# Perceiver attention: score, mask and exponentiate by pairs of batches, with half slots interleaved

## The chip, the cores and the metric

One core of one Trainium2 chip runs the whole kernel in one launch. The metric is device time in microseconds (us), as the median of several runs. Engines: TensorE (PE; PEld is its weight load), VectorE (DVE), ScalarE (ACT), GpSimd (POOL), and SyncE (SP), which issues the transfers. They run beside each other and meet only at semaphores.

## The reference

Eight layers update x, 32 batches of 128 rows of 128 values, with a context of 32 x 128 x 96. The change lies in the third attention, a Perceiver:

```python
def _L2_xattn_ref(x, latents, mask, ...):          # x: context, latents: layernorm of the running x
    xn = layernorm(x, ln_x_g, ln_x_b)
    ln = layernorm(latents, ln_l_g, ln_l_b)
    q = ln @ Wq.T
    kv = jnp.concatenate([xn @ Wkv.T, ln @ Wlkv.T], axis=1)
    k, v = (kv[..., :INNER], kv[..., INNER:])      # 2 heads of 64
    qn = rmsnorm(q, qn_g) * SCALE
    kn = rmsnorm(k, kn_g)
    attn = jnp.einsum('bhid,bhjd->bhij', qn, kn)   # 128 x 256 per batch and head
    attn = jnp.where(full_mask, attn, -max)
    attn = jax.nn.softmax(attn, axis=-1)
    out = jnp.einsum('bhij,bhjd->bhid', attn, v)
    return out @ Wo.T + bo
x = x + tanh(g_xattn[2]) * _L2_xattn_ref(ctx, _layernorm(x), mask, ...)
```

The other seven layers are cosine attention, soft mixture of experts, 16-head attention, routed experts, then after the Perceiver eight experts, another attention, and a selected GELU.

## The kernel before

The layers follow each other, with a barrier of all engines after each (`end_layer`, L63 to L67). x stays in on-chip memory (`x_resident`) throughout. The diff touches `layer4_perceiver` (L1662) alone.

There the 32 batches form eight groups of four (G = 4). Each engine has a program of its own, written out by hand as a loop over slots, `SLOTS = range(-4, 9)`. In slot t an engine works on several groups at once: statistics of group t+4, normalising and turning (transposing) of the inputs of t+3, projections of t+2, key scaling and turned q and k of t+1, scores and softmax of t, and output of t-1. `there(j)` leaves out groups that don't exist. An engine works strictly in its own order, and a wait stops all behind it.

What each step is, in the names of the profile:

- ScalarE: `keep` (L1868) copies one batch's q, k and v out of `a_project_bank` (rows a_q L1871 and a_kv L1872). `square` (L1874) squares q and k of a group (a_sq, L1879 and L1881). `empty_work` (L1891) copies a turned tile out of `a_work_bank`. `exponentiate` (L1898) does one exponential for each batch and head, eight for a group, with the row sums. `copy_turned_probs` (L1866) copies one batch's turned probabilities.
- VectorE: `mean_squares` (L1767), `scale_keys` (L1779), `mask_scores` (mask L1791 for two batches at a time, maximum L1797, `shift` L1801), `invert_sums` (L1807), `normalise_outputs` (L1812), `update` of x (L1822), and the layer norms in the helper `Norm` (L127 to L147).
- GpSimd: powers to -1/2: key roots (L1737) and query roots (L1739), `rstd` of the latent (L1744) and of the context norm (L140), and the bias added to x (L188).
- TensorE: `turn` (L1946) for q, context, latent, latent keys and context keys, all through the one bank `a_work_bank`; `turn_probs` (L1953); `project` (L1963, L1964), one batch at a time through `a_project_bank`, which `keep` must have emptied; `scores` (L1977); `weigh` (L1987); turned output (L2020) and output product (L2030) in `a_out_bank`.

`a_score_bank` holds the scores of four batches, and the turned probabilities are written to the same places. So `scores(t)` waits until all four of group t-1 have been copied (`pT_done`). In a slot TensorE turns group t-1's probabilities first, and ScalarE exponentiates group t near the end of its slot, before `square(t + 2)`:

```python
                    if there(t):
                        exponentiate(t)
                    if there(t + 2):
                        square(t + 2)
```

Context blocks are loaded by SyncE into one of two buffers as soon as the context norm has used it (L1725).

## Time and profile before

| | |
|---|---|
| median of 3 runs | 2292.95 us (2291.43 to 2298.33) |
| profiled execution, its own time | 2296.02 us |
| its span | 2294.2 us |
| TensorE / VectorE / ScalarE / GpSimd busy | 2004.6 / 1571.2 / 1250.2 / 796.4 us |
| mean granted clock of TensorE | 0.922 |
| Perceiver stage, first work to last update | 1360.6 to 1577.7 us |
| next layer's first VectorE row | 1578.77 us |

A row of a timeline gives the start in us from the span's start, the duration in us, the engine, the line, the operation, the tile written <- the tiles read, and in brackets how long the engine stood before it and for whom. Rows of one kind in a run are merged (x4). Instructions on one engine are pipelined, so the next starts somewhat before the printed end of the one before; the pitch is from start to start. A row of a stretch gives, for a:b, its length and then the busy us of each engine, and the granted clock (1.00 is 2.4 GHz, 0.50 is 1.2 GHz).

### The profile page before, as it was taken

Reading aid. Unit: us, or ns where it says so; the run is one execution under the profiler, and the core shown is the slowest. Engines: PE = TensorE matmul, PEld = TensorE weight load, DVE = VectorE, ACT = ScalarE, POOL = GpSimd, SP = SyncE. Lnnn points to the kernel's source line nnn. Section 1 sums busy time; section 2 is a strip of 40 time slices with the busy share of each in tenths; the row PEclk is TensorE's granted clock in tenths of the full one; section 3 lists DMA queues with packets and bytes.
Section 4 is the critical chain, followed back from the end, with each engine's and each line's share of the span. In section 5 each row is a group of like instructions: output and inputs, shape, how many; then the busy total and the mean of one; then the engine's idle time right before and its main releaser. Section 6 shows DMA issues by size and latency. Waiting matters only on the chain. (4 is left out here: it accounts for less than half of the span.)

```text
span 2294.2 us, 49158 instructions
## 1 busy us (share of the span) xinstructions
PE 2004.6 (87%) x18068; PEld 1514.7 (66%) x18068; DVE 1571.2 (68%) x3190; ACT 1250.2 (54%) x2832; POOL 796.4 (35%) x698
## 2 busy tenths in 40 slices
PE   6669999999996998969999977777997999999964
PEld 3359999899994666646666644665684666666653
DVE  5789999999997888734544445554575566666644
ACT  3279888888871676723333215754422566666631
POOL 1124445444461333225444444331000333333233
PEclk7589999999997999979999988997998999999975
DMA  2100000000002000044533520001000000000001
GB/s 59 43 1 8 14 9 14 9 14 15 8 8 77 9 9 6 2 92 94 123 81 75 117 42 15 4 1 52 1 1 11 1 4 5 9 4 1 1 2 37
DMA packets 41418, 61.81 MB, mean 27 GB/s; under 512 B 9464, under 2 KB 18208, under 8 KB 40800
## 3 DMA queue, kind: packets, MB, share of 16 engines
q1 hardware_dynamic: 41184, 58.66, 10.6%
q8 instruction: 151, 2.47, 0.5%
q14 instruction: 83, 0.68, 0.1%
HBM read 56.02 MB, written 2.62 MB: 26 GB/s over the span
## 5 line engine op out<-in xcount | busy, mean ns | idle before, releaser
L827 POOL TENSOR_TENSOR a_probs<-a_probs,a_rsums 128x1024 f32<-128x1024 f32 x64 | 121.3, 1896 | 321.3 <-DVE a_rsums L875 321.3
L1510 POOL TENSOR_TENSOR f_h<-f_gated,f_w_spread 128x512 f32<-128x512 f32 x128 | 161.6, 1268 | 196.7 <-DVE f_gated L1564 93.7
L1564 DVE TENSOR_TENSOR f_gated<-f_silu,f_up 128x512 f32<-128x512 f32 x128 | 87.1, 686 | 184.3 <-PE f_up L1641 169.4
L2336 ACT ACTIVATE f_combine<-f_logits,f_neg_row_max 128x128 f32<-128x128 f32 x512 | 198.5, 396 | 0.7 <-DVE f_neg_row_max L2194 0.7
L1604 ACT ACTIVATE f_silu<-f_gate 128x512 f32<-128x512 f32 x128 | 76.2, 597 | 221.2 <-PE f_gate L1641 218.0
L2155 POOL TENSOR_TENSOR f_slot_sum<-f_slot_sum,f_logits 128x512 f32<-128x512 f32 x96 | 122.7, 1278 | 182.2 <-DVE f_slot_max L2273 99.1
L2163 POOL TENSOR_TENSOR f_acc<-f_acc,f_row_factor 128x512 f32<-128x512 f32 x128 | 136.2, 1066 | 60.5 <-DVE f_slot_max L2273 38.4
L1656 PEld LDWEIGHTS f_acc<-f_down,f_h 128*128 128x128 f32 x1024 | 128.9, 192 | 42.6 <-issue 37.8
L2397 PE MATMUL f_give_bank<-f_y,f_combineT 128*128 128x128 f32 x1024 | 140.7, 281 | 12.8 <-DVE f_y L2243 7.4
L863 DVE TENSOR_REDUCE a_negmax<-a_score_bank 128x8 f32<-128x1024 f32 x64 | 78.2, 1222 | 102.9 <-PE a_score_bank L1004 102.9
L2386 PE MATMUL f_slot_bank<-f_logits,f_xn 128*128 128x128 f32 x1024 | 136.5, 276 | 6.0 <-issue 5.1
L2424 PE MATMUL f_logit_bank<-f_phi,f_xT 128*128 (+1 forms) x1024 | 137.1, 280 | 3.0 <-ACT f_logits L2316 3.0
L2397 PEld LDWEIGHTS f_give_bank<-f_y,f_combineT 128*128 128x128 f32 x1024 | 125.6, 193 | 20.2 <-DVE f_y L2243 14.9
L1641 PE MATMUL f_gate<-f_xT,f_gate_up 128*128 128x512 f32 x256 | 133.2, 602 | 2.2 <-DVE f_gated L1564 2.2
L2259 DVE TENSOR_TENSOR f_logits<-f_logits,f_neg_slot_max 128x512 f32<-128x512 f32 x128 | 131.6, 1028 | 4.4 <-ACT f_combine L2336 3.4
L1656 PE MATMUL f_acc<-f_down,f_h 128*128 128x128 f32 x1024 | 131.8, 275 | 2.5 <-POOL f_h L1510 2.5
L1641 PE MATMUL f_up<-f_xT,f_gate_up 128*128 128x512 f32 x256 | 131.6, 596 | 0.0
L2386 PEld LDWEIGHTS f_slot_bank<-f_logits,f_xn 128*128 128x128 f32 x1024 | 124.5, 192 | 7.9 <-issue 6.4
L2424 PEld LDWEIGHTS f_logit_bank<-f_phi,f_xT 128*128 128x128 f32 x1024 | 126.9, 196 | 3.6 <-ACT f_logits L2316 3.6
L2374 PE MATMUL f_expert_bank<-f_w,f_slots 128*32 128x128 f32 x4096 | 127.5, 276 | 1.2 <-issue 1.2
L2374 PEld LDWEIGHTS f_expert_bank<-f_w,f_slots 128*32 128x32 f32 x4096 | 109.5, 111 | 9.8 <-issue 2.2
L931 ACT ACTIVATE a_probs<-a_probs 128x1024 f32<-128x1024 f32 x64 | 67.8, 1060 | 70.9 <-DVE a_probs L866 70.9
(327 smaller groups left out, 4997.3 us busy)
## 6 DMA issues: line engine op xcount, KB each, us to landing
f_w_spread<-f_routing_rows SPq DMA_DIRECT2D x64, 512.0 KB, 9.9
f_w<-in_f_w SPq DMA_DIRECT2D x16, 256.0 KB, 2.5
a_cT<-in_ctxT SPq DMA_DIRECT2D x16, 192.0 KB, 2.5
f_gate_up<-in_f_guT SPq DMA_DIRECT2D x1, 2048.0 KB, 8.1
out<-x_resident SPq DMA_DIRECT2D x8, 256.0 KB, 2.4
c_cT<-in_ctxT SPq DMA_DIRECT2D x8, 192.0 KB, 2.5
a_ctx<-in_ctx SPq DMA_DIRECT2D x8, 192.0 KB, 2.6
f_phi<-in_f_phi SPq DMA_DIRECT2D x1, 1024.0 KB, 5.9
```

What stands on the lines that cost most here:

```text
L827: nc.gpsimd.tensor_tensor(probs[:, u], probs[:, u], rsums[:, u, :].unsqueeze(2).to_broadcast([S, 8, S]), ALU.mult).then_inc(normalised, 1)
L1510: nc.gpsimd.tensor_tensor(h[:, u % KEPT, :], gated[:, u % 2, :], w_spread[:, u // PER, u % PER, :], ALU.mult).then_inc(weighted, 1)
L1641: nc.tensor.matmul(ps[step % 2][:, :], gu_w[:, step, k, :], norm.xT[:, s, :], start=True, stop=True).then_inc(done, 1)
L1656: last = nc.tensor.matmul(acc[s][:, j * D:(j + 1) * D], h[:, u % KEPT, j * S:(j + 1) * S], down_w[:, u, :], start=u == 0 and j == 0, stop= ...
L2155: nc.gpsimd.tensor_tensor(slot_sum[:, :, :], slot_sum[:, :, :] if g > 1 else raw[:, (m - 1) % RING], raw[:, m % RING], ALU.add).then_inc(p ...
L2163: nc.gpsimd.tensor_tensor(acc[:, group(g), :], acc[:, group(g), :], factor[:, m // GROUPS % 3, group(g)].unsqueeze(2).to_broadcast([S, G, D]),
L2259: nc.vector.tensor_tensor(e, e, wide(neg_slot[:, m // GROUPS % 3, :]), ALU.add).then_inc(shifts, 1)
L2336: last = nc.scalar.activation(back[:, m % BACKS, j, :], raw[:, m % RING, j, :], ACT.Exp, bias=neg_row[:, k, b:b + 1], accum_out=row_part[: ...
L2374: last = nc.tensor.matmul(expert_banks[m % 2][rows, j * D:(j + 1) * D], slots[:, m % KEPT, j, rows], w_s[:, k, e, :], start=True, stop=True)
L2386: last = nc.tensor.matmul(slot_bank[:, j * CH:(j + 1) * CH], xn[:, g * G + j, :], raw[:, m % RING, j, :], start=True, stop=True)
L2397: last = nc.tensor.matmul(give_banks[m % 2][:, j * D:(j + 1) * D], backT[:, m % TURNED, j, :], y[:, m % KEPT, j, :], start=True, stop=True)
L2424: last = nc.tensor.matmul(logit_banks[m % 2][:, j * CH:(j + 1) * CH], xT[:, g * G + j, :], phi_c[:, c, :], start=True, stop=True)
```

## The change

A group's scores, masks, maxima, shifts, exponentials, turned probabilities and weighing are done for two batches at a time (p = 0, 1) instead of four, with waits to match, and the two halves stand in different places of a slot:

- TensorE scores the first pair of t at the start of slot t and turns its probabilities near the end of the same slot. The second pair is scored in mid-slot and its probabilities turned in slot t+1, behind the first weighing of t. All four projections move, so that a projection stands between most other steps.
- ScalarE exponentiates the first pair of t in mid-slot t and copies its turned probabilities late in that slot. The second pair's exponentials stand first in slot t+1.
- VectorE does the sum of squares first, then mask, maximum and shift of the first pair, then the norms (context ahead of latent), and the second pair's behind the key scaling. The shift of a pair is now its own small multiply.
- GpSimd's query roots of t+1 wait until the exponentials of t-1, which read the same buffer, are done. Before, the key roots ahead of them waited for the shift of t-1. The context norm's `rstd` stands behind the bias add.
- The conversion of the mask (`neg`) stands at the end of slot -2 instead of at the start of slot -1.

The instructions and their shapes are otherwise the same. Nothing of the diff touches another layer or the barrier ahead of the eight experts.

```diff
@@ -1732,10 +1732,10 @@
                     j = t + 1
                     if there(j):
                         pool.wait_ge(ms_done, j + 1)
-                        if j >= 2:
-                            pool.wait_ge(shift_ready, j - 1)
                         nc.gpsimd.tensor_tensor(rn[:, j % 2, 2 * G:], ms[:, 2 * G:], core.minus_half[:, 0:4 * G],
                                                 ALU.pow).then_inc(k_roots, 1)
+                        if j >= 2:
+                            pool.wait_ge(exps, G * (j - 1))
                         nc.gpsimd.tensor_tensor(rn[:, j % 2, 0:2 * G], ms[:, 0:2 * G], core.minus_half[:, 0:2 * G],
                                                 ALU.pow).then_inc(q_roots, 1)
                     if there(t + 4):
@@ -1743,9 +1743,10 @@
                         pool.wait_ge(n_l.veps_done, j + 1)
                         nc.gpsimd.tensor_tensor(n_l.rstd[:, s, :], n_l.veps[:, s, :], core.minus_half[:, 0:G],
                                                 ALU.pow).then_inc(n_l.rstd_done, 1)
-                        n_c.gpsimd_rstd(pool, i, s, j)
                     if there(t):
                         bias.gpsimd_add(pool, at(t), n_l.xn_done)
+                    if there(t + 4):
+                        n_c.gpsimd_rstd(pool, *at(t + 4))
 
             @block.vector
             def _(dve):
@@ -1782,24 +1783,21 @@
                         rn[:, s, 2 * G:].rearrange("p (n h) -> p n h", h=H).unsqueeze(3).to_broadcast([S, 2 * G, H, DH]),
                         ALU.mult).then_inc(kn_done, 1)
 
-                def mask_scores(j):
...
+                def mask_scores(j, p):
+                    s, bs = j % 2, slice(2 * p, 2 * p + 2)
+                    dve.wait_ge(scored, 2 * j + p + 1)
+                    if j >= 2:
+                        dve.wait_ge(flips, 4 * (j - 2) + 2 * p + 2)
+                    nc.vector.tensor_tensor(
+                        sc[:, s, :, bs, :].rearrange("p h b k -> p h (b k)"), score_half(p),
+                        neg[:, 4 * j + 2 * p:4 * j + 2 * p + 2].rearrange("p b c k -> p (b c k)").unsqueeze(1)
+                        .to_broadcast([S, H, 2 * 2 * S]), ALU.add).then_inc(masked, 1)
+                    dve.wait_ge(masked, 2 * j + p + 1)
+                    nc.vector.tensor_reduce(negmax[:, :, bs], sc[:, s, :, bs, :], AX.X, ALU.max, negate=True).then_inc(maxed, 1)
+                    dve.wait_ge(maxed, 2 * j + p + 1)
                     dve.wait_ge(q_roots, j + 1)
+                    nc.vector.tensor_tensor(shift[:, s, bs], negmax[:, :, bs].rearrange("p h b -> p b h"),
+                                            rn[:, s, 4 * p:4 * p + 4].rearrange("p (b h) -> p b h", h=H),
                                             ALU.mult).then_inc(shift_ready, 1)
 
                 def invert_sums(j):
...
@@ -1829,28 +1827,30 @@
                         dve.wait_ge(weights, LOADED)
                         nc.vector.tensor_scalar(q_gain[:, :], vecs[:, 4:5], DH ** -0.5, None, ALU.mult).then_inc(gain_done, 1)
                         bias.vector_start()
-                    if t == -1:
-                        nc.vector.tensor_scalar(neg[:, :, CTX, :], mask_u8[:, :, :], 1.0, MASKED, ALU.subtract, ALU.mult)\
-                            .then_inc(neg_done, 1)
+                    if there(t + 1):
+                        mean_squares(t + 1)
+                    if there(t):
+                        if t == 0:
+                            dve.wait_ge(neg_done, 2)
+                        mask_scores(t, 0)
+                    if there(t + 3):
+                        n_c.vector_normalise(dve, *at(t + 3))
+                        n_l.vector_normalise(dve, *at(t + 3))
                     if there(t - 1):
                         invert_sums(t - 1)
-                    if there(t + 1):
-                        mean_squares(t + 1)
-                    if there(t + 3):
-                        n_l.vector_normalise(dve, *at(t + 3))
-                        n_c.vector_normalise(dve, *at(t + 3))
                     if there(t + 4):
                         latent_statistics(t + 4)
                     if there(t + 1):
                         scale_keys(t + 1)
                     if there(t):
-                        if t == 0:
-                            dve.wait_ge(neg_done, 2)
-                        mask_scores(t)
+                        mask_scores(t, 1)
                     if there(t - 1):
                         normalise_outputs(t - 1)
                     if there(t + 4):
                         context_statistics(t + 4)
+                    if t == -2:
+                        nc.vector.tensor_scalar(neg[:, :, CTX, :], mask_u8[:, :, :], 1.0, MASKED, ALU.subtract, ALU.mult)\
+                            .then_inc(neg_done, 1)
                     if there(t - 1):
                         update(t - 1)
 
@@ -1861,8 +1861,8 @@
 
                 def copy_turned_probs(j, b):
                     act.wait_ge(flips, G * j + b + 1)
-                    if j and b == 0:
-                        act.wait_ge(weighed, j)
+                    if j and b % 2 == 0:
+                        act.wait_ge(weighed, 2 * (j - 1) + b // 2 + 1)
                     nc.scalar.activation(pT[:, b].rearrange("p a k -> p (a k)"), score_bank[:, 512 * b:512 * b + 512],
                                          ACT.Copy).then_inc(pT_done, 1)
 
@@ -1890,10 +1890,10 @@
                         ps = ps.rearrange("p (b k) -> p b k", b=G)
                     nc.scalar.activation(out, ps, ACT.Identity if "bias" in args else ACT.Copy, **args).then_inc(work_emptied, 1)
 
-                def exponentiate(j):
+                def exponentiate(j, p):
                     s = j % 2
-                    act.wait_ge(shift_ready, j + 1)
-                    for b in range(G):
+                    act.wait_ge(shift_ready, 2 * j + p + 1)
+                    for b in (2 * p, 2 * p + 1):
                         for h in range(H):
                             last = nc.scalar.activation(sc[:, s, h, b, :], sc[:, s, h, b, :], ACT.Exp,
                                                         bias=shift[:, s, b, h:h + 1], scale=rn[:, s, b * H + h:b * H + h + 1],
@@ -1902,34 +1902,36 @@
 
                 for t in SLOTS:
                     if there(t - 1):
-                        copy_turned_probs(t - 1, 0)
-                        copy_turned_probs(t - 1, 1)
+                        exponentiate(t - 1, 1)
                     if there(t + 1):
                         empty_work("q", t + 1, qT[:, (t + 1) % 2], scale=q_gain[:, 0:1])
+                    if there(t + 2):
+                        keep(t + 2, 0)
                     if there(t - 1):
                         copy_turned_probs(t - 1, 2)
                         copy_turned_probs(t - 1, 3)
                     if there(t + 2):
-                        keep(t + 2, 0)
+                        keep(t + 2, 1)
                     if there(t + 3):
                         empty_work("c", t + 3, cT[:, (t + 3) % 2, :], bias=vecs[0:C, 1:2], scale=vecs[0:C, 0:1])
                     if there(t + 2):
-                        keep(t + 2, 1)
+                        keep(t + 2, 2)
+                    if there(t):
+                        exponentiate(t, 0)
                     if there(t + 3):
                         empty_work("l", t + 3, lT[:, (t + 3) % 2, :], bias=vecs[:, 3:4], scale=vecs[:, 2:3])
                     if there(t + 2):
-                        keep(t + 2, 2)
+                        keep(t + 2, 3)
+                    if there(t):
+                        copy_turned_probs(t, 0)
+                        copy_turned_probs(t, 1)
                     if there(t + 1):
                         empty_work("k_lat", t + 1, kT[:, (t + 1) % 2, :, LAT, :], scale=vecs[:, 5:6])
                     if there(t - 1):
                         act.wait_ge(o_turned, t)
                         nc.scalar.activation(oT[:, :], out_bank[:, :], ACT.Copy).then_inc(oT_ready, 1)
-                    if there(t + 2):
-                        keep(t + 2, 3)
                     if there(t + 1):
                         empty_work("k_ctx", t + 1, kT[:, (t + 1) % 2, :, CTX, :], scale=vecs[:, 5:6])
-                    if there(t):
-                        exponentiate(t)
                     if there(t + 2):
                         square(t + 2)
 
...
@@ -1964,54 +1966,58 @@
                     nc.tensor.matmul(both[:, CTX, D:3 * D], cT[:, j % 2, bs], wc[:, :], start=True, stop=True)\
                         .then_inc(projected, 1)
 
-                def scores(j):
+                def scores(j, p):
                     s = j % 2
                     pe.wait_ge(work_emptied, use["k_ctx", j] + 1)
                     if j:
-                        pe.wait_ge(pT_done, G * j)
-                    for p in range(2):
-                        for b in (2 * p, 2 * p + 1):
...
-                def weigh(j, b):
-                    pe.wait_ge(pT_done, G * j + b + 1)
+                        pe.wait_ge(pT_done, G * (j - 1) + 2 * p + 2)
+                def weigh(j, p):
+                    pe.wait_ge(pT_done, G * j + 2 * p + 2)
                         pe.wait_ge(updated, j)
...
                 for t in SLOTS:
+                    if there(t):
+                        scores(t, 0)
                     if there(t - 1):
-                        turn_probs(t - 1)
+                        weigh(t - 1, 0)
                     if there(t + 1):
                         turn("q", t + 1, kept, G * (t + 1) + G, lambda b: q[:, (t + 1) % 2, b, :])
                     if there(t + 2):
                         project(t + 2, 0)
                     if there(t - 1):
-                        weigh(t - 1, 0)
-                        weigh(t - 1, 1)
+                        turn_probs(t - 1, 1)
+                    if there(t + 2):
+                        project(t + 2, 1)
                     if there(t + 3):
                         turn("c", t + 3, n_c.xn_done, t + 4, lambda b: n_c.xn[:, (t + 3) % 2, b, :], width=C)
+                    if there(t + 2):
+                        project(t + 2, 2)
                     if there(t):
-                        scores(t)
-                    if there(t + 2):
-                        project(t + 2, 1)
+                        scores(t, 1)
                     if there(t - 1):
-                        weigh(t - 1, 2)
-                        weigh(t - 1, 3)
+                        weigh(t - 1, 1)
                     if there(t + 3):
                         turn("l", t + 3, n_l.xn_done, t + 4, lambda b: n_l.xn[:, (t + 3) % 2, b, :])
                     if there(t + 2):
-                        project(t + 2, 2)
+                        project(t + 2, 3)
+                    if there(t):
+                        turn_probs(t, 0)
                     if there(t + 1):
                         turn("k_lat", t + 1, kn_done, t + 2, lambda b: kn[:, (t + 1) % 2, b, LAT, :])
                     if there(t - 1):
@@ -2019,8 +2025,6 @@
                         for b in range(G):
                             last = nc.tensor.transpose(out_bank[:, b * S:(b + 1) * S], o[:, b, :], core.ident[:, :])
                         last.then_inc(o_turned, 1)
-                    if there(t + 2):
-                        project(t + 2, 3)
                     if there(t + 1):
                         turn("k_ctx", t + 1, kn_done, t + 2, lambda b: kn[:, (t + 1) % 2, b, CTX, :])
                     if there(t - 1):
```

## Rows read from the trace of the kernel before

**Rows 1.** The page, part 1: busy us, share of the span, instructions

```profile
PE 2004.6 (87%) x18068; PEld 1514.7 (66%) x18068; DVE 1571.2 (68%) x3190; ACT 1250.2 (54%) x2832; POOL 796.4 (35%) x698
```

**Rows 2.** Busy time by stretch: slots, each from one group's first exponential on

```profile
core 0: us, PE busy (x) PEld busy (x) DVE busy (x) ACT busy (x) POOL busy (x), PEclk, DMA share, GB/s
1440.79:1463.26 22.47, 18.18 (x113) 14.07 (x112) 13.73 (x36) 14.74 (x37) 8.68 (x7) 0.92 0.04 9
1463.26:1484.51 21.25, 16.60 (x113) 13.03 (x112) 13.65 (x36) 14.86 (x38) 7.24 (x6) 1.00 0.01 1
...
1548.08:1563.61 15.53, 11.35 (x75) 9.05 (x73) 6.33 (x8) 7.19 (x23) 0.00 (x0) 0.83 0.00 0
```

**Rows 3.** Waits of six slots: who waited for whom; total, times, longest

```profile
DVE a_rsum L1807 <- ACT a_scores L1898: 27.4, 6, 8.3
```

**Rows 4.** Timeline (start us, us, engine, line, operation) of one slot, ScalarE

```profile
1463.26 0.61 ACT L1898 ACTIVATE a_scores<-a_scores,a_shift,a_rn 128x256 f32<-128x256 f32 x1
...
1467.94 0.63 ACT L1879 ACTIVATE a_sq<-a_q 128x512 f32<-128x512 f32 x1
...
1469.41 1.06 ACT L1866 ACTIVATE a_probsT<-a_score_bank 128x512 f32<-128x512 f32 x2
...
1470.36 0.68 ACT L1891 ACTIVATE a_qT<-a_work_bank,a_q_gain 128x512 f32<-128x512 f32 x1
...
1480.68 0.28 ACT L1871 ACTIVATE a_q<-a_project_bank 128x128 f32<-128x128 f32 x1 [0.30 <-PE a_project_bank L1964]
...
1481.33 0.69 ACT L1891 ACTIVATE a_kT<-a_work_bank,a_vecs 128x512 f32<-128x512 f32 x1
```

**Rows 5.** Timeline of the same slot, VectorE and GpSimd

```profile
1469.54 1.75 DVE L1767 TENSOR_REDUCE a_ss<-a_sq 128x24 f32<-128x1536 f32 x1 [1.27 <-ACT a_sq L1881]
...
1471.42 1.11 DVE L147 TENSOR_SCALAR a2l_xn<-x_resident,a2l_mean_var,a2l_rstd 128x128 f32<-128x128 f32 x4
...
1471.59 2.94 POOL L1737 TENSOR_TENSOR a_rn<-a_ms,minus_half 128x16 f32<-128x16 f32 x1 [8.37 <-DVE a_ms L1772]
...
1472.44 1.04 DVE L147 TENSOR_SCALAR a2c_xn<-a_ctx,a2c_mean_var,a2c_rstd 128x96 f32<-128x96 f32 x4
...
1474.91 1.23 DVE L1779 TENSOR_TENSOR a_kn<-a_kv,a_rn 128x1024 f32<-128x1024 f32 x1
...
1476.05 2.35 DVE L1791 TENSOR_TENSOR a_scores<-a_score_bank,a_neg 128x1024 f32<-128x1024 f32 x2
...
1478.32 2.33 DVE L1797 TENSOR_REDUCE a_negmax<-a_scores 128x4 f32<-128x1024 f32 x2
...
1480.69 0.17 DVE L1801 TENSOR_TENSOR a_shift<-a_negmax,a_rn 128x8 f32<-128x8 f32 x1
```

**Rows 6.** Timeline of the same slot, TensorE

```profile
1474.12 2.00 PE L1977 MATMUL a_score_bank<-a_kT,a_qT 64*128 64x256 f32 x16
...
1477.23 1.89 PE L1987 MATMUL a_out_bank<-a_kv,a_probsT 128*128 128x64 f32 x16
...
1478.96 0.61 PE L1946 MATMUL a_work_bank<-ident,a2l_xn 128*128 128x128 f32 x4
...
1479.40 0.81 PE L1963 MATMUL a_project_bank<-a_w_lat,a2l_xT 128*128 128x384 f32 x2
...
1480.05 0.60 PE L1964 MATMUL a_project_bank<-a_w_ctx,a2c_xT 96*128 96x256 f32 x2
```

**Rows 7.** Busy time by stretch (columns as in rows 2), around one fall of the clock

```profile
1455.00:1489.30 34.30, 26.90 (x178) 21.05 (x176) 19.67 (x50) 24.24 (x63) 10.40 (x9) 0.99 0.00 1
1489.30:1494.00 4.70, 4.67 (x22) 3.92 (x22) 3.39 (x9) 4.68 (x9) 1.18 (x1) 0.64 0.00 0
```

**Rows 8.** Timeline: opening and end of the stage

```profile
1401.31 0.64 ACT L1879 ACTIVATE a_sq<-a_q 128x512 f32<-128x512 f32 x1
...
1418.26 1.28 ACT L1898 ACT_TABLE_LOAD   x1
...
1576.99 0.75 DVE L1822 SCALAR_TENSOR_TENSOR x_resident<-a_out_bank,gates,x_resident 128x512 f32<-128x512 f32 x1 [3.57 <-PE a_out_bank L2030]
```

50 lines of the change are left out of this document (18 added, 32 removed).

## Prediction, before the changed kernel was run

> **What bounds the kernel now.** I read the page first, then the trace by stretches. TensorE is busy 87% of the span [rows 1], but that is a mean over eight layers, and the change touches one of them, the Perceiver attention, which runs from 1360.6 us to its last update at 1576.99 + 0.75 = 1577.7 us [rows 8]. I cut that stage at the start of each group's exponentials, which gives its slots [rows 2]: 22.47, 21.25 and, the last, 15.53 us for three of the seven (the other four have the same pattern). In the 21.25 us slot no engine is full: TensorE 16.6, VectorE 13.65, ScalarE 14.86, GpSimd 7.24. So the slot is set by a chain through several engines, and the view of waits says where it is handed on: VectorE waits 27.4 us in six slots for a group's last exponential [rows 3].
>
> Following one slot in time order [rows 4, 5]: ScalarE does eight exponentials 1463.26 to 1467.94 = 4.68 us, then squares until 1469.41 = 1.47 us. In that time TensorE only turns probabilities as they come, and VectorE waits for the squares. VectorE then sums squares from 1469.54, normalises both inputs from 1471.42, does latent statistics and keys, masks from 1476.05, takes maxima from 1478.32, and gives the shift at 1480.69. ScalarE meets the shift only behind the last projection and key copies, and the next exponentials start at 1484.51 [rows 2]. The next slot's exponentials therefore can't start before all four batches of this one have gone round: exponentials, squares, VectorE's block, masks, copies, one behind the other.
>
> **The change part by part.** The sum of the work stays, save one small shift multiply more per slot. Pitches, from the start of a row to the start of the next on its engine:
> - TensorE [rows 6]: 16 score rows 1474.12 to 1476.04 = 1.92; 16 weighing rows 1477.23 to 1478.96 = 1.73; one turn of four 0.44; one projection 0.65 (1479.40 to 1480.05) and 0.44 = 1.09. A slot: scores 1.92, weighing 2 x 1.73, four projections 4.36, five turns 2.2, turned probabilities 1.76, turned output 0.44, output product about 0.9 = 15.0 us.
> - ScalarE [rows 4]: exponentials 4.68, squares 1.47, two probability copies 0.95 (1469.41 to 1470.36), one keep 0.65 (1480.68 to 1481.33), the other copies 0.5 to 0.7. A slot: 14.2 us.
> - VectorE [rows 5]: sums 1.9, latent and context normalise 1.0 and 0.95, keys 1.15, masks 2.3, maxima 2.35, the rest about 4.3: 14 us. GpSimd 8.7 us [rows 2].
>
> So the floor is about 15 us, and the question is the ring of waits that the new order makes. I laid the new order out by hand with these pitches and 0.05 to 0.15 us for a hand-off between engines (sum of squares 1469.54 starts 0.1 after the squares). Time 0 is the end of ScalarE's squares in a full slot.
> - VectorE: sums to 2.0; mask, maximum and shift of the first pair 1.2 + 1.2 + 0.2, to 4.7; context normalise to 5.6 (now ahead of the latent one); latent normalise 6.7; latent statistics 8.2; keys 9.4 (GpSimd's key roots, 2.94 [rows 5], come at 5.0, covered by 3.2 us); mask to shift of the second pair 12.1; output 12.7; context statistics 14.0; update 16.1.
> - TensorE: weighs the first pair to 1.35, turns q 1.8, projects 2.9, turns the second pair's probabilities to 3.8 (their exponentials end at 2.4, so nothing waits), projects from 3.9 to 5.0, waits for the context normalise, turns it 5.7 to 6.15, projects 7.2, second scores 8.2, second weighing 9.9, latent turn 10.35, projects 11.4, turns the first pair 12.35, latent keys 12.8, output 13.2, context keys 14.0 to 14.45 (behind ScalarE's copy of the latent keys), output product 15.3, first scores of the next slot 16.3.
> - ScalarE: second exponentials 0 to 2.3, q 2.9, keep 3.1 to 3.8, two probability copies 4.8, keep 5.8, context copy 6.4 to 7.0, keep 8.0, first exponentials of the slot's own group 10.4 (their shift came at 4.7, covered by 3.3 us), latent copy 11.0, keep 12.3, copies 13.3, latent keys 13.8, output 14.3, context keys 15.2, squares 16.7.
>
> The ring closes at **16.7 us**, where the undisturbed slot of before took 21.25. It runs squares, sums, first mask and shift, context normalise, then down TensorE's queue to the turned first pair, and back over ScalarE's copies. TensorE waits 0.7 us ahead of the context turn and 0.8 us ahead of the context keys. Moving GpSimd's context root behind the bias add costs nothing: it waits for VectorE's context statistics at 14.0 and is wanted at 4.7 of the next slot. GpSimd's query roots now wait for the second exponentials (2.4) and would have started at 5.0 anyway. The mask conversion of all batches stays between the same two VectorE steps. What is queued behind the earlier shift wait on ScalarE is q's copy and the keeps; that wait is over by 4 us.
>
> Whole stage. *Opening*: squares of group 1 end at 1401.31 + 1.6 = 1402.9 [rows 8]. Projections that stood behind turns move into waits and the context normalise comes first, which I take as 3 us over two slots (bounds 0 and 4). From 1399.9: 5.7 to the context turn, 0.5 turn, 2.2 projection at the low clock (twice 1.09), 0.7 keep, 1.28 table load [rows 8], which gives the first exponentials at 1410.4 instead of 1419.5; 8.1 more to the end of squares, 1418.5. *Four full slots* 66.8, to 1485.3. *Slot 5*, without turns of new inputs: 16.0. *Slot 6*, without projections: first exponentials at 4.7, mask, output, keys and copies behind, 11.4, to 1512.7. *Slots 7 and 8*: the chain of group 6's update, 12.7, then weighing, turning, weighing, normalising and output of group 7, 9.3: 22.0, to 1534.7. Against 1577.7 that is 43.0 us less. The slots 22.47 (granted clock 0.92) and 21.25 (1.00) have the same work [rows 2]; a spell at the low clock cost 1.2 us. I add 1 us for each of five slots: **38 us**. The profiled execution took 2296.0 us, 3.1 above the median 2292.95 of the three runs; from the median, 2292.95 - 38 = **2255 us**. The ends: 45 us (spells vanish, opening at its best) and 30 us (opening at nothing, hand-offs 0.1 us longer on about ten of the ring), so 2248 to 2263 for this case.
>
> **The rivals.**
> - *The clock keeps falling in short waits.* The stage's clock is 0.99 to 1.00 where TensorE is fed, and 0.64 from 1489.3 to 1494, right behind the exponentials in which it only turned [rows 7]. That stretch holds about 3.4 us at 1.2 GHz and loses half of it, 1.7 us. Before, idle time elsewhere took most of it in; now TensorE has 15.0 of 16.7 us of work, and nothing takes it in. Twice in each of five slots: 17 us, saving 26, **2267 us**. For it: two waits remain in each slot. Against: each is under 1 us, and the long thin phase is gone.
>
> The Trainium skill (TensorE: Matmul & The Clock Gate, section "A second HAM failure mode: psum-queue depth-cycling") says that a TensorE that idles briefly between groups of matmuls can swing between the clock levels and lose time in each burst. By that rule the time would be this rival's 2267 and not 2255; this case's stretches at 1.00 with short waits inside [rows 7] speak against it.
>
> - *The hand-offs cost more than I laid out.* Two halves double the crossings between masks, exponentials, turns and copies. Before, they lay inside the one long wait and cost nothing. If the ring takes 19 us instead of 16.7, five slots lose 11.5: saving 27, **2266 us**.
> - *The halves don't overlap.* The second exponentials still stand at the head of ScalarE's slot, ahead of the keep that the next projection wants. If TensorE has nothing to do under them, the slot stays near 21 us: **2290 us**. Against: 1.35 + 0.45 + 1.1 = 2.9 us of work without a wait lie under 2.3 us.
> - *Slower.* The one mechanism that I find is the clock in the dense stage. At 1.2 GHz TensorE's 15.0 us of a slot become 30. With a share s of its work at the low level a slot takes about 16.7 + 15 s; this passes 21.5 us at s = 0.32. At s = 0.5, 24.2 against 21.5 in six slots is 16 us more: **2309 us**. The stage shows 0.83 at worst in a slot [rows 2], the thinnest one.
>
> **How the numbers follow.** Forecast 2255 us with a chance of 0.72 (2248 to 2263); clock rival 0.10 and hand-off rival 0.10 (2266, 2267); no overlap 0.04; slower 0.04. The range 2246 to 2271 takes in the first three. A measurement of this kernel can tell some 0.3%, 7 us, from no change: faster 0.92, same 0.04, slower 0.04.
>
> **What would show it.** Right: slots of 16.5 to 18 us from one group's first exponential to the next's; TensorE over 85% busy in them at a clock of 0.95 or more; exponentials in two blocks of four; the first at about 1410 us; VectorE's longest wait no longer for ScalarE; the last update near 1539. Wrong: waits of TensorE for the context normalise or key copies far over 1 us, a clock of 0.8, or a slot that VectorE's queue sets. Layers before and behind should keep their lengths; if they don't, the difference isn't this mechanism.

## The result, and the profile after

| | before | after |
|---|---|---|
| median | 2292.19 us (4 runs, 2289.72 to 2298.33) | 2263.95 us (4 runs, 2261.06 to 2269.13) |
| ratio | | 0.9878, 95% interval 0.9859 to 0.9897 |
| profiled execution, its span | 2296.02, 2294.2 us | 2269.13, 2267.0 us |
| Perceiver stage | 1360.63 to 1577.74 = 217.1 us | 1359.88 to 1549.12 = 189.2 us |

28 us less, where 38 were forecast (2255 us, range 2246 to 2271). The time lies inside the range, but 1 us above the 2248 to 2263 of the forecast case itself and nearer to the rivals' 2266 and 2267 us, so only the traces can tell these apart. The profiled execution after was the slowest of its four, 5.2 us above their median. In the two traces the stage alone gives 27.9 us, and the layers ahead and behind kept their lengths to within 1.5 us. The page's first part, against [rows 1]:

```profile
PE 2001.4 (88%) x18068; PEld 1512.6 (67%) x18068; DVE 1574.4 (69%) x3198; ACT 1252.2 (55%) x2832; POOL 802.1 (35%) x698
```

The work is the same; VectorE has eight instructions more (the shifts). Busy time by stretch of the kernel after, with the columns of [rows 2] (the number in brackets is how many instructions). A slot is now counted from one group's second block of exponentials to the next's, as ScalarE's slot begins with it:

```profile
1418.68:1439.35 20.67, 19.50 (x116) 15.71 (x114) 13.95 (x37) 15.01 (x38) 8.91 (x6) 0.85 0.04 10
1439.35:1456.84 17.49, 16.53 (x114) 12.96 (x114) 13.98 (x37) 15.01 (x37) 8.92 (x6) 1.00 0.05 13
...
1491.82:1508.91 17.09, 15.49 (x106) 12.19 (x106) 9.75 (x12) 13.46 (x35) 5.75 (x3) 1.00 0.00 1
1531.65:1549.12 17.47, 13.30 (x60) 11.85 (x60) 2.40 (x4) 4.23 (x12) 0.00 (x0) 0.57 0.00 1
```

Three full slots take 17.49 us each, where 20.9 to 22.5 stood before (two of them in [rows 2]), and TensorE is busy 16.5 of them. The slot ahead of them took 20.67 us at a clock of 0.85. The last row is the stretch from the last block of exponentials to the last update: 17.47 us at 0.57. Before, the stretch from the last four exponentials to the last update took 11.8 us, in another order and at a clock of 0.79:

```profile
1565.94:1577.74 11.80, 9.33 (x60) 8.19 (x58) 2.39 (x4) 4.96 (x15) 0.00 (x0) 0.79 0.00 1
```

The timeline of one full slot after, in the order of time, against [rows 4 to 6]:

```profile
1456.84 0.59 ACT L1898 ACTIVATE a_scores<-a_scores,a_shift,a_rn 128x256 f32<-128x256 f32 x1
...
1460.23 0.28 ACT L1871 ACTIVATE a_q<-a_project_bank 128x128 f32<-128x128 f32 x1 [0.38 <-PE a_project_bank L1966]
...
1461.05 0.91 PE L1965 MATMUL a_project_bank<-a_w_lat,a2l_xT 128*128 128x384 f32 x2
...
1461.43 1.04 DVE L147 TENSOR_SCALAR a2c_xn<-a_ctx,a2c_mean_var,a2c_rstd 128x96 f32<-128x96 f32 x4
...
1462.53 0.64 PE L1948 MATMUL a_work_bank<-ident,a2c_xn 128*96 128x128 f32 x4
1462.61 0.59 ACT L1872 ACTIVATE a_kv<-a_project_bank 128x512 f32<-128x512 f32 x1
...
1463.25 0.30 PEld L1965 LDWEIGHTS a_project_bank<-a_w_lat,a2l_xT 128*128 128x128 f32 x2 [0.33 <-ACT a_kv L1872]
1463.25 0.91 PE L1965 MATMUL a_project_bank<-a_w_lat,a2l_xT 128*128 128x384 f32 x2
...
1464.53 1.14 PE L1978 MATMUL a_score_bank<-a_kT,a_qT 64*128 64x256 f32 x8
...
1465.29 0.60 ACT L1898 ACTIVATE a_scores<-a_scores,a_shift,a_rn 128x256 f32<-128x256 f32 x1
...
1465.59 2.00 PE L1989 MATMUL a_out_bank<-a_kv,a_probsT 128*128 128x64 f32 x16
...
1467.43 0.61 PE L1948 MATMUL a_work_bank<-ident,a2l_xn 128*128 128x128 f32 x4
...
1469.15 0.28 ACT L1871 ACTIVATE a_q<-a_project_bank 128x128 f32<-128x128 f32 x1 [0.30 <-PE a_project_bank L1966]
...
1471.61 0.63 PE L1948 MATMUL a_work_bank<-ident,a_kn 128*128 128x128 f32 x4 [0.75 <-ACT a_kT L1891]
1472.08 1.09 PE L2034 MATMUL a_out_bank<-a_wo,a_oT 128*128 128x128 f32 x8
...
1473.10 1.14 PE L1978 MATMUL a_score_bank<-a_kT,a_qT 64*128 64x256 f32 x8
```

With 1456.84 as time 0 the layout can be read against it. VectorE's context normalise begins at 4.6 (laid out 4.7) and the context turn at 5.7 (5.7). The first exponentials of the slot's own group start at 8.45 (8.0). But the projection behind the context turn starts at 6.4 where 6.15 was laid out, just after the second keep's copy (1462.61 + 0.59 = 1463.20) has ended. What TensorE waits for there is that keep, not the context normalise. From there the layout slips on, to 16.0 for the squares (15.2) and 17.5 for the end (16.7).

### The profile page after: what moved, and what is told of

Same layout as the page of the kernel before. It is cut to its first block and busy times, and to the rows that moved or that the text cites. A ratio compares the mean times of both kernels' runs of the same rounds, so it can differ in the third digit from the quotient of the medians.

```text
span 2267.0 us, 49188 instructions
## 1 busy us (share of the span) xinstructions
PE 2001.4 (88%) x18068; PEld 1512.6 (67%) x18068; DVE 1574.4 (69%) x3198; ACT 1252.2 (55%) x2832; POOL 802.1 (35%) x698
## 3 DMA queue, kind: packets, MB, share of 16 engines
q8 instruction: 151, 2.47, 0.4%
## 5 line engine op out<-in xcount | busy, mean ns | idle before, releaser
L2401 PE MATMUL f_give_bank<-f_y,f_combineT 128*128 128x128 f32 x1024 | 141.0, 281 | 11.8 <-DVE f_y L2247 7.5
```

Of the source, the lines that this page charges most:

```text
L2401: last = nc.tensor.matmul(give_banks[m % 2][:, j * D:(j + 1) * D], backT[:, m % TURNED, j, :], y[:, m % KEPT, j, :], start=True, stop=True)
```

## Experiments

The slot lengths below are read from traces like the one above. In a kernel the full slots behind the first agree to 0.02 us where the clock is 1.00, so one trace tells 0.1 us in a slot, far less than a time can. Times of single executions aren't compared, because the stage itself began anywhere from 1353 to 1363 us in these traces, with the same code ahead of it.

**Pairs alone, in the old places.** The half groups with their own waits, but VectorE, ScalarE and TensorE in the order of before. On ScalarE (the other two engines' lines are left out here):

```diff
-                        exponentiate(t - 1, 1)
...
-                        exponentiate(t, 0)
...
+                        exponentiate(t, 0)
+                        exponentiate(t, 1)
```

> The changed kernel's half groups (mask, maximum, shift, exponentials, turned probabilities and weighing by pairs, each pair with its own waits), but every step back in the place of the kernel before, the two pairs one behind the other. Theory: the gain comes from putting the two pairs in different places of a slot, not from the pairs as such. Before, the exponentials started 3.6 us after the shift was ready, so an earlier shift is worth nothing: slots 20.9 to 22.5 us as before, and a time of 2285 to 2296 us. Rival: the finer waits alone let the pairs overlap; then slots of 18 to 19 us and about 2270 us.

Measured: 2293.75 us, ratio to before 1.0014 (0.9998 to 1.0029). One of its slots:

```profile
1438.35:1460.05 21.70, 17.91 (x113) 14.24 (x112) 14.12 (x37) 14.86 (x37) 7.96 (x6) 0.92 0.04 10
```

The finer waits, and GpSimd's part of the change, which this kernel kept, give nothing. The gain comes from the new order. That order moves three things at once, at the least: the two pairs, the projections with their keeps, and VectorE's norms (worth 0.7 us in a slot, as the second of the next three edits shows). No run moves the steps without splitting the group, and that rival stands. Before, the shift was ready at 1480.69 + 0.17 = 1480.86 and the exponentials started at 1484.51 [rows 5, 2]: 3.65 us, in which ScalarE did two keeps and three other copies. An order of whole groups that moved them out of that place could therefore win up to 3.65 us in a slot (an estimate from these rows), where the change won 3.8 (21.25 to 17.49). That splitting alone isn't enough is shown; that it is needed isn't.

**Which ring closes the slot: three edits.** The first puts the context normalise ahead of the first mask:

```diff
+                    if there(t + 3):
+                        n_c.vector_normalise(dve, *at(t + 3))
                     if there(t):
                         mask_scores(t, 0)
                     if there(t + 3):
-                        n_c.vector_normalise(dve, *at(t + 3))
                         n_l.vector_normalise(dve, *at(t + 3))
```

> The changed kernel with VectorE's context normalise ahead of the first pair's mask, so that the context turn can start 2.6 us earlier in a slot. Theory of the prediction: the ring runs over sums, first mask and shift, context normalise and the context turn; then a full slot falls from 17.49 by 0.5 to 1.0 us. Rival, read from the trace after: TensorE's own queue with the keep copies sets the slot, and the context turn has only some 0.3 us to spare on the next projection; then a full slot falls by 0 to 0.3 us.

The second puts the latent normalise ahead of the context one:

```diff
-                        n_c.vector_normalise(dve, *at(t + 3))
                         n_l.vector_normalise(dve, *at(t + 3))
+                        n_c.vector_normalise(dve, *at(t + 3))
```

> The changed kernel with VectorE's latent normalise ahead of the context one again, as before the change: the context turn can start 1.1 us later. Theory of the prediction (the normalise lies in the ring): 17.49 becomes about 18.6 us. Rival (TensorE's queue is the ring, the context turn has 0.3 us to spare): about 18.3 us. If neither holds, 17.5.

The third turns q twice:

```diff
+                        for b in range(G):
+                            nc.tensor.transpose(work_bank[:, b * S:(b + 1) * S], q[:, (t + 1) % 2, b, :], core.ident[:, :])
                         turn("q", t + 1, ...)
```

> The changed kernel with q turned twice in each slot: four more 128x128 turns, 0.44 us of TensorE, between the first weighing and the first projection. Theory of the prediction: TensorE waits ahead of the context turn anyway, so 0.44 us there is hidden and a full slot stays at 17.5 us. Rival (TensorE's queue and the keeps behind it are the ring from there on): a full slot grows by 0.4 us to 17.9.

One full slot of each, in this order:

```profile
1431.41:1448.91 17.50, 16.34 (x114) 13.06 (x114) 13.98 (x37) 14.90 (x38) 8.90 (x6) 1.00 0.05 13
```

```profile
1440.35:1458.52 18.17, 16.27 (x114) 12.96 (x114) 14.06 (x37) 15.01 (x37) 8.90 (x6) 1.00 0.05 12
```

```profile
1441.09:1459.02 17.93, 16.77 (x118) 13.48 (x118) 14.00 (x37) 15.02 (x38) 8.91 (x6) 1.00 0.05 12
```

An earlier context normalise gives 0.0, and one that starts 1.03 us later in the slot (5.62 us in, against 4.59) costs 0.68, so it has 0.35 us to spare: it isn't in the ring. In the first of the three the context turn did come sooner, and the projection behind it still waited for the keep, at the same 6.42 us into the slot:

```profile
1437.83 0.91 PE L1966 MATMUL a_project_bank<-a_w_lat,a2l_xT 128*128 128x384 f32 x2 [0.42 <-ACT a_kv L1873]
```

0.44 us more on TensorE ahead of it costs 0.44, all of it. My ring over the sums, the first mask and the context normalise falls; in this part the ring runs down TensorE's queue and the keep copies.

**The copy wait ahead of the context keys.** TensorE stood 0.75 us there. The latent keys' turn goes ahead of the turned probabilities, and their copy ahead of the probability copies:

```diff
+                        empty_work("k_lat", t + 1, ...)
                         copy_turned_probs(t, 0)
                         copy_turned_probs(t, 1)
-                        empty_work("k_lat", t + 1, ...)
...
+                        turn("k_lat", t + 1, ...)
                         turn_probs(t, 0)
-                        turn("k_lat", t + 1, ...)
```

> The changed kernel with the turn of the latent keys ahead of the turned probabilities of the first pair on TensorE, and their copy ahead of the probability copies on ScalarE. In a full slot of the trace after TensorE stands 0.75 us for that copy before the context keys. Theory (TensorE's queue with its copies sets the slot): the wait goes, and a full slot falls from 17.49 to 17.0 to 17.2 us; four slots give 1 to 2 us. Rival: the ring is closed elsewhere; then 17.5 us stays.

Measured: full slots of 17.49 us behind the first, unchanged; 2264.94 us, ratio 0.9868 (0.9829 to 0.9908), not to be told from the changed kernel. The wait did go from the context keys, but came back one step later:

```profile
1468.08 0.73 ACT L1891 ACTIVATE a_kT<-a_work_bank,a_vecs 128x512 f32<-128x512 f32 x1
1468.28 0.97 PEld L2034 LDWEIGHTS a_out_bank<-a_wo,a_oT 128*128 128x128 f32 x8 [0.88 <-ACT a_oT L1932]
1468.29 1.16 PE L2034 MATMUL a_out_bank<-a_wo,a_oT 128*128 128x128 f32 x8 [0.64 <-ACT a_oT L1932]
```

The last keep of that slot starts at 1465.43, so 2.86 us lie between it and the output product; after, 1469.15 to 1472.08 = 2.93 us. ScalarE does a keep, two probability copies, a key copy and one more in that time in either order. The miss formed a second theory: these copies belong to the ring. The next kernel adds one edit to this one, the output's copy between the two probability copies:

```diff
                         copy_turned_probs(t, 0)
+                        nc.scalar.activation(oT[:, :], out_bank[:, :], ACT.Copy).then_inc(oT_ready, 1)
                         copy_turned_probs(t, 1)
-                        nc.scalar.activation(oT[:, :], out_bank[:, :], ACT.Copy).then_inc(oT_ready, 1)
```

> The kernel with the latent keys first, and on ScalarE the copy of the turned output between the two probability copies instead of behind them. Theory formed from the last run: the slot is set by ScalarE's four copies between the last keep and the output product (2.93 us in the changed kernel, 2.86 with the latent keys first, where TensorE's wait only moved to the output product), then TensorE's queue of output product, scores, weighing, q and projections, and the keeps. The output product then starts 0.4 us sooner, and a full slot falls from 17.49 to 17.0 to 17.2 us. Rival: the slot is held by something else that neither order touches; 17.49 stays.

```profile
1436.00:1453.10 17.10, 16.64 (x114) 12.91 (x113) 13.98 (x37) 14.98 (x37) 8.91 (x6) 1.00 0.05 13
...
1527.17:1539.86 12.69, 8.61 (x60) 7.39 (x58) 2.40 (x4) 4.12 (x12) 0.00 (x0) 0.84 0.01 1
```

Four slots of 17.08 to 17.10 us. The output product started 2.47 us behind the last keep (1448.28 to 1450.75) instead of 2.86, and the slot is shorter by the same 0.39 us against the kernel with the latent keys first. So this stretch lies in the ring.

**GpSimd's edit undone**, the context root ahead of the bias add:

```diff
+                        n_c.gpsimd_rstd(pool, i, s, j)
                     if there(t):
                         bias.gpsimd_add(pool, at(t), n_l.xn_done)
-                    if there(t + 4):
-                        n_c.gpsimd_rstd(pool, *at(t + 4))
```

> The changed kernel with one edit undone: GpSimd's root of the context norm ahead of the bias add again. Theory of the prediction: the move costs and gives nothing, as the bias is wanted only by the update at the slot's end; slots of 17.49 us as before. Rival: the bias add then waits for the context statistics (13.8 us into the slot), ends some 16.4 us in, and pushes the update, at 16.4, by 0 to 0.3 us, which TensorE's weighing waits for: slots up to 17.8.

```profile
1433.31:1450.81 17.50, 16.54 (x114) 12.98 (x114) 13.98 (x37) 15.02 (x38) 8.89 (x6) 1.00 0.05 13
```

17.50: that part of the change is worth nothing in these slots. But little room is left: the bias add now started at 1448.66 and took 1.27 us, to 1449.93 by its row, and the update started at 1449.75 (ends of GpSimd's rows are rough), 0.1 us behind the output product as in the kernel after.

**The low clock in the first slot and at the end.** Five stretches of the kernel after, two ahead of and in the first full slot and three at the stage's end:

```profile
1414.00:1417.00 3.00, 1.03 (x8) 0.58 (x6) 0.31 (x4) 2.19 (x5) 1.22 (x2) 1.00 0.00 0
1421.00:1424.50 3.50, 3.50 (x14) 2.89 (x14) 3.43 (x9) 0.80 (x3) 3.50 (x2) 0.50 0.00 0
...
1531.65:1533.90 2.25, 1.16 (x8) 0.97 (x8) 0.75 (x1) 2.25 (x9) 0.00 (x0) 1.00 0.00 0
1533.90:1537.00 3.10, 3.03 (x15) 3.06 (x15) 0.20 (x1) 0.18 (x2) 0.00 (x0) 0.52 0.02 5
1537.00:1541.00 4.00, 3.31 (x16) 2.91 (x16) 0.00 (x0) 1.20 (x2) 0.00 (x0) 0.50 0.00 0
```

Both times TensorE had stood idle for about half of a stretch or more, still at 1.00 (1.03 us busy of 3.00, 1.16 of 2.25), and soon behind it ran at 0.50. To test whether these waits matter, spare turns of the identity, which nothing reads, stand ahead of TensorE's waits, first in the last two slots, then, in another kernel, in the opening:

```diff
+                def spare_turns(bank, n):
+                    for k in range(n):
+                        nc.tensor.transpose(bank[:, (k % 4) * S:(k % 4 + 1) * S], core.ident[:, :], core.ident[:, :])
...
+                        if t >= GROUPS - 1:
+                            spare_turns(work_bank, 6)
                         pe.wait_ge(oT_ready, t)
```

> The changed kernel with spare turns of the identity (nothing reads them) in TensorE's waits of slots 7 and 8: 4 to 8 of 0.11 us ahead of the weighings, the output turn and the output product of the last two groups. Theory: the tail ran 6.0 us over my layout because TensorE worked at 1.2 GHz from 1533.9 us on, after short waits; with the waits filled the granted clock of the last 15 us is near 1.00, the stretch from the last block of exponentials to the last update falls from 16.7 us to 11 to 12, and the time by 4 to 6 us. Rival: turns don't hold the clock, or it was another thing: then the clock stays at 0.5 to 0.7 there, and the spare turns add up to 1 us.

> The changed kernel with spare turns in TensorE's waits of the opening (slots -1, 0 and the head of slot 1, 6 to 16 of 0.11 us each). Theory: slot 1 took 20.67 us against 17.49 in the next three because TensorE ran at half clock from 1417 to 1424.5, as slot 0 left it idle; filled, the second slot takes 17.5 to 18 us, the first exponentials start up to 1.5 us sooner, and the time falls by 3 to 5 us. Rival: the fall of the clock doesn't hang on these waits; then slot 1 stays at 20 us or more, or the fall moves to a later slot, with no gain.

The expectation's 16.7 us runs to the start of the last update, 1548.37; to its end it is the 17.47 of above, and the rows below are counted so too. The stretch from the last exponentials' block to the last update with the spare turns in the tail; then, without them there, of the kernel with the busy opening and of the one with the extra turn:

```profile
1524.29:1536.34 12.05, 10.88 (x90) 9.78 (x88) 2.40 (x4) 4.12 (x12) 0.00 (x0) 1.00 0.01 1
```

```profile
1525.52:1538.30 12.78, 8.56 (x60) 7.49 (x60) 2.40 (x4) 4.11 (x12) 0.00 (x0) 0.90 0.00 0
```

```profile
1535.15:1547.53 12.38, 8.16 (x60) 7.09 (x60) 2.39 (x4) 4.11 (x12) 0.00 (x0) 0.93 0.00 0
```

The tail at 1.00 takes 12.05 us, with 30 spare turns in it, 5.4 less than after. But the code of that stretch without spare turns also ran in 12.38 and 12.78 us at 0.93 and 0.90, and elsewhere in 17.22 at 0.58. So 5.1 of the 17.47 us are a price of the clock (TensorE's busy time is 13.30 us at 0.57 and 8.16 at 0.93 for the same 60 rows), and whether it falls due differs between the traces. The times, 2260.62 us with the ratio 0.9855 (0.9816 to 0.9893) and 2261.30 us with 0.9857 (0.9817 to 0.9897), can't be told from the changed kernel's 0.9878.

The opening is clearer. The first full slot with spare turns ahead of it:

```profile
1415.80:1433.21 17.41, 16.45 (x114) 12.89 (x113) 13.87 (x37) 15.03 (x37) 8.92 (x6) 1.00 0.05 12
```

17.41 us. In the seven kernels with neither spare turns there nor the latent keys first (the changed kernel, both norm orders, the extra turn, the tail order, the busy tail, GpSimd's edit undone) that slot took 20.66 to 22.10 us at a low clock for part of it. (In two of them, the one with the latent norm first and the one with the extra turn, a full slot takes 18.17 and 17.93 at 1.00 anyway.) But in the two with the latent keys first it took 16.95 and 17.08 at 1.00 without spare turns, and TensorE had stood idle at least as much ahead of it there. The stretch from the first exponentials to the first full slot with the latent keys first, and in the kernel after:

```profile
1410.69:1418.18 7.49, 4.02 (x29) 2.81 (x27) 3.32 (x11) 7.32 (x17) 3.09 (x4) 1.00 0.01 3
```

```profile
1410.52:1418.68 8.16, 5.61 (x32) 3.77 (x32) 3.58 (x11) 7.35 (x18) 1.59 (x3) 0.92 0.01 3
```

TensorE was busy 4.02 of 7.49 us in the one that kept the clock and 5.61 of 8.16 in the one that lost it. So spare turns go with the high clock in the opening, but idle time alone doesn't tell when it falls, and why the latent-keys order kept it isn't shown.

**The order in the last slot.** The first weighing of group 7 goes behind the turned probabilities of its second pair, in that slot alone:

```diff
-                    if there(t - 1):
+                    if there(t - 1) and there(t):
                         weigh(t - 1, 0)
...
                         turn_probs(t - 1, 1)
+                    if there(t - 1) and not there(t):
+                        weigh(t - 1, 0)
```

> The changed kernel, and in the very last slot alone the first weighing of group 7 stands behind the turned probabilities of its second pair instead of ahead of them. In the trace after, TensorE waited there until 1533.9 us for the update of group 6, weighed for 3.4 us, turned for 1.1 to 1.9 us and waited another 0.7 us for the copies before the second weighing. Theory: that order costs 1.5 to 2.5 us once, as the copies can run under the first weighing; from the last block of exponentials to the last update 16.7 becomes 14.5 to 15.5 us at the same clock. Rival: the turned probabilities now wait for the exponentials as long as they gained, and the tail stays within 0.5 us.

```profile
1522.18:1533.78 11.60, 8.59 (x60) 7.50 (x60) 2.40 (x4) 4.11 (x12) 0.00 (x0) 0.89 0.01 1
```

11.60 us at a clock of 0.89, against 12.78 at 0.90 in the kernel with the busy opening, which has the old order there: 1.2 us, less than the 1.5 to 2.5 expected.

**Together.** Two kernels put these edits together, with the new copy order and without it; both leave out the spare turns ahead of the last group's weighings:

> The kernel with the output copy sooner, the last slot's first weighing behind the turned probabilities, and spare turns of the identity in TensorE's waits of the opening and of the last two output steps. Theory: slots of 17.1 us, none at a low clock, and a tail of 10 to 11.5 us; the stage 176 to 179 us instead of 189.2, the time 8 to 12 us under the changed kernel's. Rival: the spare turns and orders get in each other's way, and it isn't faster than the same kernel without the new copy order.

> The changed kernel with the last slot's first weighing behind the turned probabilities and the spare turns of the opening and of the last two output steps, and nothing else. Theory: first full slot 17.4 us, the others 17.49, a tail of 10.5 to 11.5 us, granted clock 1.00 from the first exponentials to the last weighing; the stage 177 to 180 us, the time 7 to 11 us under the changed kernel's. Rival: the low clock comes from what the power of the earlier stages leaves and not from the waits; then a slot over 19 us or a tail over 13 stays somewhere.

```profile
1433.79:1450.89 17.10, 16.64 (x114) 12.91 (x113) 13.98 (x37) 14.99 (x38) 8.91 (x6) 1.00 0.05 13
...
1524.96:1535.76 10.80, 8.80 (x72) 7.70 (x70) 2.39 (x4) 4.11 (x12) 0.00 (x0) 1.00 0.00 0
```

```profile
1419.97:1437.38 17.41, 16.45 (x113) 12.88 (x113) 13.87 (x37) 15.02 (x37) 8.91 (x6) 1.00 0.05 12
...
1529.70:1540.51 10.81, 9.25 (x74) 8.03 (x72) 2.40 (x4) 4.10 (x12) 0.00 (x0) 1.00 0.00 0
```

| | stage | median | ratio to before |
|---|---|---|---|
| changed kernel | 189.2 us | 2263.95 us | 0.9878 (0.9859 to 0.9897) |
| all, with the new copy order (rows first) | 176.3 us | 2255.33 us | 0.9826 (0.9804 to 0.9849) |
| all, without it (rows second) | 177.5 us | 2252.95 us | 0.9820 (0.9798 to 0.9841) |

Both beat both kernels, and the intervals lie just clear of the changed kernel's (0.9849 and 0.9841 against 0.9859). Which of the two is better the times don't tell; the copy order's 1.2 us in the stage is below what they can show. I expected 8 to 12 and 7 to 11 us: by the ratios it is 12 and 13 us, by the stages 13.0 and 11.8 us. The stages flatter: the 189.2 us hold the slow tail of that one execution, and the kernel with GpSimd's edit undone, with the same full slots and no spare turns, took 182.8.

## Why the prediction was right, and where it was off

**The sign, the place and the mechanism held.** The full slots fell from 21.25 to 17.49 us with the new order, while the pairs alone changed nothing. Whether the order needs the split is argued, not shown. Of the edits that were costed at nothing, GpSimd's root is the one that was tried by itself, and it was worth nothing; the key and query roots' new waits were in the kernel of pairs in the old places, at no gain. TensorE had no wait under the second exponentials, so the no-overlap rival fell, as did the rival of a dense stage at half clock: the three full slots after the first ran at 1.00 with TensorE 94% busy. The first exponentials came at 1410.52 us, where 1410.4 was laid out, and VectorE's longest wait in a full slot is now for TensorE's output product (2.42 and 2.70 us ahead of two updates).

The number owes something to luck. The rows below miss by 15.2 us in sum, and an allowance of 5 us that was meant for other slots takes a third of that back. And the range was wide enough for both rivals of 2266 and 2267 us, so the time alone couldn't have told the forecast from them.

**Four terms of the sum were off.** Forecast lengths, from the prediction's own timetable, against the trace after:

| stretch | forecast | measured | difference |
|---|---|---|---|
| stage start to first full slot | 57.9 | 58.8 | +0.9 |
| first full slot | 16.7 | 20.67 | +4.0 |
| next three | 50.1 | 52.5 | +2.4 |
| slot 5 | 16.0 | 17.1 | +1.1 |
| slot 6 | 11.4 | 11.6 | +0.2 |
| the rest | 22.0 | 28.6 | +6.6 |
| clock allowance | 5.0 | (in the rows above) | -5.0 |

The sum is 10.2 us, with rounding the 38 forecast less the 27.9 measured in this pair of traces. By the medians the miss is 9 us (2263.95 against 2255).

- *The ring's size and its path.* 17.49 against 16.7 in a slot. The number was 5% off, and half of the path was wrong: I took it over the squares and VectorE's first block, where the latent-first run shows 0.35 us to spare. The way back over ScalarE's copies was right. By the trace, the path is output product, first scores, first weighing, q, projection, keep, projection, keep, projection, second scores and weighing, latent turn, projection, keep, ScalarE's copies, and back to the output product. Two parts of it were tested by an edit, the one between first weighing and first projection (+0.44 for 0.44) and the last copies (-0.39 for 0.39); the rest is read from the rows, each of which starts as the one before it on the path ends. The mis-sizing sits in the pitches: I took half of 16 score rows as 0.96 us and 16 weighing rows as 1.73 [rows 6]. In the trace after a half of scores takes 1.06 (1464.53 to 1465.59) and the weighing behind it 1.84 (1465.59 to 1467.43). Twice each in a slot that is 0.4 of the 0.8 us. Of the other 0.4, the projection ahead of the second scores took 1.28 (1463.25 to 1464.53) where I had 1.09, and the output product 1.02 (1472.08 to 1473.10) where I had about 0.9: another 0.3. There was a sign of it: [rows 2] give 16.60 us of TensorE in the slot whose pitches I summed to 15.0, and the slot after has 16.53. Had I followed the keeps, which wait for each projection and hold the next, the context wait would have shown as covered.
- *The clock.* Of my 5 us of allowance I spread 1 us over each slot. It came as about 3.2 us in the first full slot (20.67 against 17.49) and some 5 in the last 17.5 us, and none between. The price of 1.2 us was also read from too few slots. Two others of the kernel before ran at 0.84 and 0.92 and weren't longer than the 21.25 us at 1.00, so there the low clock added nothing that the slot shows:

```profile
1419.56:1440.79 21.23, 19.11 (x112) 15.02 (x112) 12.89 (x35) 14.97 (x37) 7.24 (x6) 0.84 0.04 10
1484.51:1505.39 20.88, 18.09 (x113) 14.36 (x112) 11.38 (x19) 14.84 (x37) 6.49 (x4) 0.92 0.01 1
```

  The clock rival (17 us, two falls in each of five slots) named the right cause in the wrong place: dense slots with one wait of 0.75 us and 0.2 us in shorter ones (17.49 less 16.53) kept 1.00. The falls came right behind the stretches that still leave TensorE idle, the opening and the last group's chain. The sum had these at the high clock, except one projection.
- *Slot 5.* I took 0.7 us off for the missing turns; they aren't worth more than 0.4 (17.49 to 17.09), and the ring's 0.8 us error stands in it too.
- *The hand-off rival* (19 us a slot) lay on the other side of the truth from my layout: 17.49 is a third of the way to it.

The rule cited in the prediction from the Trainium skill (TensorE: Matmul & The Clock Gate, section "A second HAM failure mode: psum-queue depth-cycling"), that TensorE idling briefly between groups of matmuls can swing the clock, isn't borne out in the full slots, which kept 1.00 with their short waits. The two falls shown above came behind longer idling, so no run here speaks for that rule.

**What stays open.** Whether the split is needed, or an order of whole groups would do as well. Why the tail ran at clocks from 0.57 to 0.93 in the nine kernels with this change that had no spare turns there (none reached 1.00), and why two orders of the opening kept 1.00 without them. The spare turns went with 1.00 in all three kernels that had them in the tail, and in all three that had them in the opening, each seen in one trace. The times don't separate the two kernels that had one of them alone from the changed kernel.

## What to carry to other kernels

When a group's work runs in one ring through all engines, halves of it that stand half a slot apart can shorten the slot; here splitting without moving gave nothing. Lay the new order out by hand, but follow each buffer's emptying copy as a wait of its own, since here the ring that closed the dense slot ran through the fullest engine and the copies that free its bank. Cost the first slot and the last chain at either clock, for that is where TensorE still stands idle, and here the low one cost 3 and 5 us.

## What the hardware showed unexpectedly

The same 60 TensorE rows at the end of the stage took 8.16 us of busy time in one kernel's trace and 13.30 in another's, at granted clocks of 0.93 and 0.57, with no change in that code; the stretch took 12.38 or 17.47 us. Once it had fallen in the tail, the clock stayed at 0.50 to the stage's end, though TensorE was busy 3.31 of 4.00 us there. The four executions of the changed kernel lie 8.1 us apart (2261.06 to 2269.13), and the stage began at 1353.1 to 1363.1 us with the same code ahead of it. On a kernel of this length an edit of 1 us in a slot is measured by its slots in the trace, not by the time.
